# First attention: low and high halves of the values in one tile, two matmul passes, output products of a batch in one turn

## The reference, cut to what matters

```python
q = (x @ Wq.T).reshape(B, T, 16, 32).transpose(0, 2, 1, 3)      # k and v likewise; x is the layernorm of the input
att = einsum('bhtd,bhsd->bhts', q, k) / sqrt(32) + causal_mask
w = softmax(att, axis=-1)
z = einsum('bhts,bhsd->bhtd', w, v).transpose(0, 2, 1, 3).reshape(B, T, D)
x = x + z @ Wo.T
```

## Time and profile before

| | |
|---|---|
| median of 3 runs | 1908.64 us (1906.13 to 1909.9) |
| profiled execution, its own time | 1907.17 us |
| its span | 1905.7 us |
| TensorE busy in it | 1805.5 us (95%) |
| VectorE / ScalarE / GpSimd busy | 1113.3 / 807.4 / 1010.0 us |
| mean granted TensorE clock | 0.986 |
| first attention | from 0 to 250.7 us of the span; its loop from 34.2 us on |

### The profile page before, as it was taken

The page is one execution under the profiler, slowest core; times in us unless marked ns, Lnnn a source line. Parts: engine busy times, 40 slices in busy tenths (PEclk is TensorE's granted clock), DMA queues, the critical chain, the costliest instruction groups (busy, mean ns, idle before and its releaser), DMA issues. The chain is left out here.

```text
span 1905.7 us, 30804 instructions
## 1 busy us (share of the span) xinstructions
PE 1805.5 (95%) x10161; PEld 1565.8 (82%) x10167; DVE 1113.3 (58%) x2769; ACT 807.4 (42%) x2063; POOL 1010.0 (53%) x965
## 2 busy tenths in 40 slices
PE   7999989999999999999888999999999999999996
PEld 5888858788999999899667888888888888867795
DVE  6676785763333333335766666666666757566345
ACT  3767633222222222221256566666665433543231
POOL 3444341397883957895457456456453203116783
PEclk9999999999999999999999999999999999999998
DMA  3556430236653645554343234233331210012666
GB/s 116 173 155 205 144 138 0 78 145 226 231 199 126 214 144 180 191 153 127 90 112 95 68 92 117 57 89 93 84 78 56 74 50 1 24 50 84 213 214 195
DMA packets 104551, 232.54 MB, mean 122 GB/s; under 512 B 20672, under 2 KB 20928, under 8 KB 101328
## 3 DMA queue, kind: packets, MB, share of 16 engines
q1 hardware_dynamic: 84080, 144.31, 25.0%
q0 software_dynamic: 19744, 85.47, 13.6%
q10 hardware_dynamic: 576, 0.79, 0.2%
HBM read 126.23 MB, written 57.93 MB: 97 GB/s over the span
## 5 line engine op out<-in xcount | busy, mean ns | idle before, releaser
L712 POOL TENSOR_SCALAR a_E<-a_E,a_inv 128x128 f32<-128x128 f32 (+3 forms) x384 | 213.9, 575 | 237.7 <-DVE a_inv L848 237.7
L745 ACT ACTIVATE a_E<-a_E,a_top 128x512 f32<-128x512 f32 (+3 forms) x384 | 211.1, 565 | 6.0 <-DVE a_top L842 5.9
L153 PE MATMUL bank<-f_UH,f_XH 128*128 x596 | 200.5, 336 | 8.4 <-POOL f_UL L165 3.4
L153 PE MATMUL bank<-f_UL,f_XH 128*128 x596 | 193.2, 324 | 0.0
L153 PE MATMUL bank<-f_UH,f_XL 128*128 x596 | 193.2, 324 | 0.0
L842 DVE CUSTOM_DVE_ANT_0 a_E<-a_causal,bank 128x512 f32<-128x512 bf16 (+3 forms) x384 | 163.6, 480 | 43.0 <-PE bank L1023 31.5
L153 PE MATMUL bank<-a_PHL,a_VH 128*128 128x512 f32 (+3 forms) x768 | 181.1, 325 | 0.9 <-issue 0.6
L737 ACT ACTIVATE a_PHL<-bank 128x512 fp32r<-128x512 f32 (+1 forms) x288 | 131.0, 528 | 112.6 <-PE bank L1039 112.5
L1821 ACT ACTIVATE f_HH<-bank 128x256 fp32r<-128x256 f32 x220 | 59.8, 323 | 232.2 <-PE bank L2218 232.1
L165 DVE TENSOR_TENSOR a_PHL<-bank,a_PHL 128x512 fp32r<-128x512 f32 (+1 forms) x288 | 153.2, 585 | 5.1 <-ACT a_PHL L737 4.8
L1876 DVE TENSOR_TENSOR f_gate<-bank,f_gate 128x352 f32<-128x352 f32 x79 | 41.3, 522 | 192.1 <-PE bank L153 192.0
(11 more groups left out here) (407 smaller groups left out, 4864.8 us busy)
## 6 DMA issues: line engine op xcount, KB each, us to landing
f_uraw<-f_up POOLq DMA_DIRECT2D x18, 1408.0 KB, 6.7
f_xb<-table SPq DMA_DIRECT2D x86, 256.0 KB, 3.2
table<-f_ob SPq DMA_DIRECT2D x86, 256.0 KB, 2.7
table<-a_zeros SPq DMA_DIRECT2D x31, 512.0 KB, 4.3
f_draw<-f_down POOLq DMA_DIRECT2D x27, 512.0 KB, 4.5
a_g<-a_f SPq DMA_DIRECT2D x160, 64.0 KB, 2.0
a_raw<-a_qkv SPq DMA_DIRECT2D x36, 256.0 KB
f_uraw<-f_up POOLq DMA_DIRECT2D x9, 704.0 KB, 4.4
```

Of the source, the lines that this page charges most:

```text
L153: m = pe.matmul(out, a, b, start=first and i == 0 and j == 0, stop=last and i == n - 1 and j == 2, skip_group_check=not check)
L712: e.tensor_scalar(self.E[sl][:, a], self.E[sl][:, a], self.inv[:, sl, i:i + 1], 0.0, ALU.mult, ALU.add).then_inc(*self.s_nrm.up(N, m - 1, i))
L745: x = e.activation(E, E, ACT.Exp, scale=-1.0, bias=self.top[:, sl, i:i + 1], accum_out=self.total[:, sl, i:i + 1])
```

## The change

- The low part of a head's values no longer has a tile of its own: it goes into the same tile `VH`, 64 columns away from the high part. One matmul with this tile gives both the high values' and the low values' product, in different rows of the bank. So the values take two passes (`PH`, `PL`) in place of three. (The product low x low comes with it.)
- Heads 0 and 1 have rows 0 to 63, heads 2 and 3 rows 64 to 127; the other half of the bank holds their low products. So the bank is emptied after every second head, by ScalarE with two copies of 64 rows (`QH`, and `S` from the other half), a turn later by VectorE with a low part into `R`, and after the fourth head GpSimd adds `R + S` into `QL`.
- VectorE's low part moves from the end of turn m (job m-3) to turn m (job m-4), behind the reciprocal and ahead of `PL`. GpSimd's addition stands ahead of its normalizing instructions.
- The projected values are staged in a tile of their own (`W`).
- `FILL`: all four output products of a batch go into the turn of "T"; before, they stood in pairs in the two turns behind it. Output weights are split in turn 0 of the next step, not in turn 6; the queries' weights are loaded 2 turns ahead, not 4.
- The memset of `VL` goes for this attention. The second attention (heads 64 wide) keeps the old form.

```diff
+        self.beside = 4 * hd <= P
+        self.VH = sb("VH", [heads, NT, P], F32R)
+        if self.beside:
+            self.VL, self.HALF = self.VH, P // 2
+            self.S, self.R, self.W = sb("S", [T]), sb("R", [T]), sb("W", [T])
...
-            self.FILL = [[("P", K, 1), ("O", 0, -1), ("O", 1, -1)], [("P", 0, 1), ("O", 2, -1), ("O", 3, -1)],
-                         [("P", V, 1)], [("T", 1)], [("P", K, 0, 1), ("O", 4, -1), ("O", 5, -1)],
-                         [("P", 0, 0, 1), ("O", 6, -1), ("O", 7, -1)], [("P", V, 0, 1)], [("T", 0, 1)]]
-            self.SPLIT = {2: (K, 1), 3: (0, 1), 5: (V, 1), 6: (self.wt, 0)}
-            self.LEAD = {K: 3, 0: 4, V: 2, self.wt: 2}
+            self.FILL = [[("P", K, 1)], [("P", 0, 1)], [("P", V, 1)],
+                         [("T", 1)] + [("O", g, -1) for g in range(TT)],
+                         [("P", K, 0, 1)], [("P", 0, 0, 1)], [("P", V, 0, 1)],
+                         [("T", 0, 1)] + [("O", g, -1) for g in range(TT, NT)]]
+            self.SPLIT = {0: (self.wt, -1), 2: (K, 1), 3: (0, 1), 5: (V, 1)}
+            self.LEAD = {K: 3, 0: 2, V: 2, self.wt: 2}
...
-        for z in (self.VH, self.VL):
+        for z in (self.VH,) if self.beside else (self.VH, self.VL):
             e.memset(z[:, :, :, :].bitcast(F32), 0.0)
...
+            if self.beside and 4 <= m < self.M + 4 and self.jobs[m - 4][3] == self.heads - 1:
+                j, b, r, h = self.jobs[m - 4]
+                e.wait_ge(*self.s_olo.after(N, j, r, b, self.half(h)))
+                e.tensor_tensor(self.QL[:, r, b * T:b * T + T], self.R[:, :], self.S[:, :], ALU.add).then_inc(
+                    *self.s_rest.up(N, j, r, b))
...
-            if 3 <= m < self.M + 3 and self.jobs[m - 3][3] == self.heads - 1:
+            if 3 <= m < self.M + 3 and self.closes(self.jobs[m - 3][3]):
                 j, b, r, h = self.jobs[m - 3]
+                own, bank = self.rows(h), self.k.bank[self.OB]
                 e.wait_ge(*self.s_av.after(N, m - 3))
-                e.activation(self.QH[:, r, b * T:b * T + T], self.k.bank[self.OB][:, :], ACT.Copy).then_inc(
-                    *self.s_ohi.up(N, j, r, b))
+                x = e.activation(self.QH[own, r, b * T:b * T + T], bank[own, :], ACT.Copy)
+                if self.beside:
+                    if m - 3 >= self.heads:
+                        e.wait_ge(*self.s_rest.after(N, *self.outputs_before(m - 3)))
+                    x = e.activation(self.S[own, :], bank[self.other_rows(h), :], ACT.Copy)
+                x.then_inc(*self.s_ohi.up(N, j, r, b, self.half(h)))
...
+            if self.beside and 4 <= m < self.M + 4 and self.closes(self.jobs[m - 4][3]):
+                self._dve_low_values(m - 4)
...
-                t = product(e, self.k.bank[self.OB][:, sblk * P:T],
-                            [(self.VH[:, h, b * TT + sblk, :], self.VL[:, h, b * TT + sblk, :])],
-                            [(self.PH[m % 2][:, a], self.PL[m % 2][:, a])],
-                            first=h == 0 and sblk == 0, last=h == self.heads - 1 and ci == 2)
+                V, p = (b * TT + sblk), m % 2
+                passes = [(self.VH[:, h, V, :], self.PH[p][:, a]), (self.VH[:, h, V, :], self.PL[p][:, a])]
+                if not self.beside:
+                    passes.append((self.VL[:, h, V, :], self.PH[p][:, a]))
...
-        if h == self.heads - 1:
-            emptied[self.OB] = self.s_olo.after(N, j, r, b)
+        if self.closes(h):
+            emptied[self.OB] = self.s_olo.after(N, j, r, b, self.half(h))
```

More of the change, by code:

```diff
@@ L507, in split @@
             c, ahead = self.SPLIT[n]
-            if j + ahead < self.STEPS:
+            if 0 <= j + ahead < self.STEPS:
                 of.append((j + ahead, c))
@@ L544, in plan @@
         self.slot, self.free, self.fill_bank, self.score_bank = {}, {}, {}, {}
-        freed, ring, self.staged = [[], []], 0, {}
+        freed, turned, ring, self.staged = [[], []], [], 0, {}
         for m in self.loops:
@@ L563, in plan @@
                             continue
+                    if c == self.vt and self.beside:
+                        self.staged[j, b], self.free[x[1:]] = self.W[:, :], turned
+                        turned = [self.s_vt.after(N, j, b)]
+                        continue
                     s = self.slot[x[1:]] = len(self.slot) % 2
@@ L595, in plan @@
                 self.s_av.plan((N, m))
-                if h == self.heads - 1:
-                    self.s_ohi.plan((N, j, r, b))
-                    self.s_olo.plan((N, j, r, b))
+                if self.closes(h):
+                    self.s_ohi.plan((N, j, r, b, self.half(h)))
+                    self.s_olo.plan((N, j, r, b, self.half(h)))
+                if self.beside and h == self.heads - 1:
+                    self.s_rest.plan((N, j, r, b))
     def moves(self, j, c, b):
@@ L614, in moves, with half, opens, closes @@
                 [(self.KH[up, 1, a], g[dn, :]), (self.KH[dn, 1, a], g[dn, :]), (self.KL[dn, 1, a], f[dn, :])]]
+    def half(self, h):
+        return h * self.hd // self.HALF
+    def opens(self, h):
+        return h * self.hd % self.HALF == 0
+    def closes(self, h):
+        return (h + 1) * self.hd % self.HALF == 0
+    def rows(self, h):
+        return slice(self.half(h) * self.HALF, (self.half(h) + 1) * self.HALF)
+    def other_rows(self, h):
+        return slice((1 - self.half(h)) * self.HALF, (2 - self.half(h)) * self.HALF)
+    def low_columns(self, cs):
+        if not self.beside:
+            return cs
+        at = (cs.start + self.HALF) % P
+        return slice(at, at + self.hd)
+    def outputs_before(self, m):
+        j, b, r, h = self.jobs[m - self.heads]
+        return j, r, b
+    def outputs_low(self, j, b):
+        if self.beside:
+            return self.s_rest.after(self.name, j, self.queries[-1], b)
+        return self.s_olo.after(self.name, j, self.queries[-1], b, self.half(self.heads - 1))
     def out_weights(self, x, r):
@@ L866, in dve, with _dve_low_values @@
                 self._dve_low_rotated(m - 1)
[L867 to L872, removed]
+            if not self.beside and 3 <= m < self.M + 3 and self.closes(self.jobs[m - 3][3]):
+                self._dve_low_values(m - 3)
+    def _dve_low_values(self, m):
+        e, N, (j, b, r, h) = self.k.dve, self.name, self.jobs[m]
+        own, a, key = self.rows(h), slice(b * T, b * T + T), (N, j, r, b, self.half(h))
+        e.wait_ge(*self.s_ohi.after(*key))
+        if self.beside and m >= self.heads:
+            e.wait_ge(*self.s_rest.after(N, *self.outputs_before(m)))
+        to = self.R[own, :] if self.beside else self.QL[own, r, a]
+        low_part(e, to, self.k.bank[self.OB][own, :], self.QH[own, r, a]).then_inc(*self.s_olo.up(*key))
     def _stats(self, loaded, tiles):
@@ L995, in _pe_fill @@
                 if g % TT == 0:
-                    e.wait_ge(*self.s_olo.after(N, j, self.queries[-1], g // TT))
+                    e.wait_ge(*self.outputs_low(j, g // TT))
                 a = slice(g * P, g * P + P)
@@ L1049, in _pe_values @@
             e.wait_ge(*self.s_vlo.after(N, j, b))
-        if h == 0 and self.OB in emptied:
+        if self.opens(h) and self.OB in emptied:
             e.wait_ge(*emptied[self.OB])
@@ L1055, in _pe_values @@
                 a = slice(self.P_AT[sblk], self.P_AT[sblk] + T - sblk * P)
-                t = product(e, self.k.bank[self.OB][:, sblk * P:T],
-                            [(self.VH[:, h, b * TT + sblk, :], self.VL[:, h, b * TT + sblk, :])],
-                            [(self.PH[m % 2][:, a], self.PL[m % 2][:, a])],
-                            first=h == 0 and sblk == 0, last=h == self.heads - 1 and ci == 2)
+                V, p = (b * TT + sblk), m % 2
+                passes = [(self.VH[:, h, V, :], self.PH[p][:, a]), (self.VH[:, h, V, :], self.PL[p][:, a])]
+                if not self.beside:
+                    passes.append((self.VL[:, h, V, :], self.PH[p][:, a]))
+                for x, (values, weights) in enumerate(passes):
+                    t = e.matmul(self.k.bank[self.OB][:, sblk * P:T], values, weights,
+                                 start=self.opens(h) and sblk == 0 and x == 0,
+                                 stop=self.closes(h) and ci == 2 and x == len(passes) - 1)
         t.then_inc(*self.s_av.up(N, m))
-        if h == self.heads - 1:
-            emptied[self.OB] = self.s_olo.after(N, j, r, b)
+        if self.closes(h):
+            emptied[self.OB] = self.s_olo.after(N, j, r, b, self.half(h))
     def projections_done(self):
```

7 lines of the change are left out of this document (5 added, 2 removed).

## The result

The changed kernel takes 1915.34 us in the median (13 runs, 1907.89 to 1917.29), the kernel before beside it 1908.5 us (13 runs). The ratio is 1.0036, with a 95% interval of 1.0024 to 1.0047: slower by 6.8 us. The profiled execution took 1916.62 us around a span of 1915.4.

A forecast was written before the change was run, and what follows sets the result against it. TensorE was taken to bound the first attention's loop. Gains of 2.7 (four full groups), 1.2 (up to 105 us), 1.0 (end) and 0.1 (start) sum to 5.0 us, giving 1903.6 us; range 1895 to 1912.

The forecast's parts named there:

- The bound: First attention's loop: TensorE sets the pace, busy 26.7 of 27 us at full clock; removed matmuls gain until the next engine limits.
- the third pass: Values' product in each turn: the four VL matmuls go, 0.63 us each, 20.3 us of TensorE's issue over 32 turns.
- The short turn: Turn that turns the values: the fourth product waits for their bank, freed by VL; turn 8.45 or 9.04 us, some 2.6 waiting.
- the first kind: First short turn of a step, keeping the queries' weight copy (0.59): fourth product starts at +7.1 us, turn 9.04.
- the S copy: Second ScalarE copy of 64 partitions in the outputs' evacuation: taken as 0.49 us, with 0 and 1.0 as ends.
- The clock: Short turn's new wait of 2.3 to 2.9 us: forecast A had the clock hold, 1903.6 us, chance 0.45.
- right at the first kind: New wait of 2.3 to 2.9 us likened to idle times of 2.65 and 2.70 us, after which the clock was not full.
- rival C: Clock falls at all five short-turn waits and stays low through the next projection, 2.3 us each; 1915 us, chance 0.14.
- the query weights' load: Sync queue in the first step: this load now stands ahead of the query moves, costing 0.5 us.
- The first step: Turns from 54.33 to 78.44, without products: 0.63 us less each, counted as 2.7 us gained up to 78.44.
- The tail: From turn 28 to the stage's end: 37.4 us against 38.4, gain 1.0, possibly a loss of 3.
- The start: Removed memset of VL: TensorE's first projection waits for YL on VectorE, not GpSimd; gain 0 to 0.2 us, taken as 0.1.

The follow-up runs named there:

- after with two memsets: Changed kernel with two memsets of a spare tile on GpSimd at the start, where the memset of VL stood; ratio 1.0028.
- the kernel of 1895.67: Changed kernel with products ahead of turned values, weights loaded earlier and the next stage's fetch in turn 27 instead of 20; 1895.67 us, ratio 0.9935.
- both repairs of the loop: Changed kernel with eight constant matmuls ahead of each short turn's fourth product and earlier weight loads; 1907.85 us, ratio 1.0003.
- two memsets in the best kernel: The kernel of 1895.67 with two memsets of a spare tile on GpSimd at the start; ratio 0.9939.
- with the two repairs: Both repairs of the loop, here with two memsets of a spare tile on GpSimd at the start as well; ratio 1.0004.

## Why the prediction was wrong, step by step

**The bound.** Right: TensorE sets the pace in the loop. A turn with one projection takes 5.75 to 5.77 us, forecast 5.78; the third pass is worth its 0.63 a turn wherever nothing else is late.

**The short turn, without the clock.** Right, closely. The wait for the bank of the turned values is in all five short turns, put down to VL on VectorE. The fourth product starts 6.58 us after the turn's start at 128.75 (forecast 6.5), and in the first kind 7.70 us after 100.13 (forecast 7.1; 0.6 more, as the output weights come late). With the clock held and the loads early the turns are 8.66 and 9.17 (forecast 8.45 and 9.04), and four groups take the 104.3 us forecast. Against it, the S copy takes its full place (0.60 between QH and S, 0.62 to PH) rather than 0.49, some 0.2 us on that chain.

**The clock: the step that failed.** The text had both rows for it, waits of 2.65 and 2.70 with a fall and one of 1.50 without, put the new wait at 2.3 to 2.9 us "right at the first kind", and still gave the fall at all five 0.14, because TensorE is busy on both sides of the wait. Being busy around it did not help: the clock fell at each of the five, down to waits of 2.16 us, and again at each of the five in the profile of after with two memsets. Its price was less than rival C's 2.3 us each: with the loads early the five short turns take 10.51, 10.13, 10.54, 9.46 and 10.21 us, and with the waits filled as well 9.18, 8.66, 9.16, 8.67 and 8.67. That is 1.3 to 1.5 for each of the four with a fall; the one of 9.46 had none, and most of its 0.8 is the wait for moved queries. Where the low clock reaches the next turn, up to 0.65 more (turns of 6.40 and 6.27 instead of 5.75). From turn 8 to 28 filling the waits brought 7.4 us in after and 6.8 with the loads early. C's 2.3 us came from the matmuls at 36.51, taken as the first fall lasting on. Three stretches of before (columns of the earlier trace rows) show two falls, with the full clock between them:

```profile
28.40:31.70 3.30, 2.82 (x12) 2.42 (x12) 0.62 (x2) 0.80 (x2) 0.00 (x0) 0.50 0.81 199
31.80:35.10 3.30, 1.78 (x11) 1.30 (x11) 3.30 (x9) 2.06 (x7) 0.00 (x0) 1.00 0.42 150
35.20:38.50 3.30, 3.11 (x7) 2.38 (x8) 2.22 (x9) 2.07 (x7) 0.00 (x0) 0.50 0.02 5
```

The rule in the Trainium skill, "TensorE: Matmul & The Clock Gate", section "HAM oscillation — how this bites in real kernels", that a loop can pay a fall in each iteration, is what the trace shows here. The page's example waits some 3 to 5 us each time; here waits of 2.16 us had a fall too.

**What was not looked at: the loads behind the query moves.** The forecast costed the query weights' load ahead of the moves, 0.5 us, and this was right: turn 1 to turn 4 takes 14.88 us instead of 14.32. It did not ask what stands behind the moves. The output weights, now split in turn 0 of the next step, are loaded behind 12 moves of some 0.6 us each, and ScalarE waits 13.8 us for them in three places, 3.9 us for other weights in three more. What it adds: a fourth product that waits 3.27 and 3.55 us instead of 2.68, a turn 9 of 7.15 instead of 5.75, and most of what the first step lost (next point). Alone its repair brought 1.0036 - 1.0015 = 0.2%, some 4 us, with intervals that overlap; together with the clock 0.33%, some 6.3, and there the intervals lie apart.

**The first step.** Forecast: 2.7 us gained by turn 8, measured 0.4 (38.4 to 38.0). Turn 4 takes 7.22, as before, although the pass that went is worth 0.63. Its clock is full (1.00 from 52 to 70 us). Behind its wait for the moves, which grew from 0.44 to 2.20, stands a second one of 1.10 (0.52 in before) for the bank of the turned values, and ahead of both ScalarE had waited for the queries' weights:

```profile
54.59 0.63 ACT L844 ACTIVATE a_WH<-a_raw 128x512 fp32r<-128x512 f32 x1 [2.35 <-DMA a_raw<-a_qkv]
60.36 0.47 PE L153 MATMUL bank<-YH,a_WH 128*128 128x512 f32 x1 [1.10 <-DVE a_VH L164]
```

With the loads ahead both ScalarE's wait and the second wait are gone, turn 4 takes 5.87, and turn 1 to turn 8 takes 36.2, 1.9 of the 2.3 us that were missing. The short turn without products takes 4.42 instead of 3.47: its values start at 79.04 behind 0.73 us of idle time, 0.10 after the low part `R` has left the outputs' bank (the trace names no releaser). That low part was moved a turn later, and the prediction booked only what that relieves.

**The tail.** Forecast 37.4, measured 37.7, with VectorE's additions 1.32 us apart (the six gaps from 252.24 to 260.15) as it said. The gain of 0.8 is there.

**The start.** That TensorE's first projection waits for YL and not for GpSimd is true, but looked one step too late: the chain to YL begins with a centring on VectorE which GpSimd, free of its memset, now holds up. Forecast 0.1 gained, measured 2.4 us lost at turn 1: 1.2 at the first scores, of which the late transposes are 0.24 and the rest goes with a longer idle time and the low clock behind it, and 1.2 in turn 0, which stays open. On the SBUF side the Trainium skill, "SBUF — State Buffer", section "🔬 SBUF: two separate sides", says that VectorE and GpSimd share one pair of ports as an exclusive lock, held for a whole instruction by whoever starts first, where VectorE runs in a mode that uses both ports or, against a GpSimd instruction that reads SBUF, takes two inputs from SBUF. In which mode the centring runs no row tells. The rows of the kernel of 1895.67 agree: the centring that starts 0.27 us after GpSimd lasts 1.28 us and ends at 12.24, behind GpSimd's instruction that began at 10.69.

**The sum.** The stage's forecast end was 245.7, the measured 260.88. The 15.2 us lie in: start 2.4, first step 2.3, turns 8 to 12 2.8, turns 12 to 28 7.4, tail 0.3. Falls of the clock and late loads share the loop's part of it. With both repairs of the loop the time from turn 1 to the end is 206.4 us, against 210.7 in before and 205.7 forecast, and the eight matmuls too many in turn 31 are in it. Of the rivals, C gave the mechanism and the sign. That its 1915 is the time measured is partly chance: its price for a fall was too high, and the late loads and the start, which no rival had, made up for it. The range of 1895 to 1912 missed the time because it held C only by half and the loads not at all.

## What to carry to other kernels

Before work is gathered into one turn, list the banks it takes in order and ask who frees each: where the last entry of a turn needs the bank that the first one took, swapping the entries can repair it, worth 0.55% here. Cost a new idle stretch of TensorE by the nearest rows of waits and the clock behind them, and if the wait is as long as one that ends in a low clock, count that as the likely case. When a load's issue turn changes, read the queue for what now stands ahead of it and for what is removed in front of other engines, even where an engine's end is far from any bound.

## What the runs showed of the hardware

- In the loop, TensorE's waits for the turned values' bank had half the clock in or behind them in 6 of 6 cases at 2.68 to 3.62 us, in 8 of 10 at 2.16 to 2.19, and in 2 of 4 at 1.90 to 1.93. Waits for moved queries had it before turn 24 at 2.03 and 2.28, and at turn 4 in none of four at 2.19 to 2.22 and in one of seven at 1.65 to 1.67. Waits of up to 1.43 for a bank in the short turns, with and without constant matmuls ahead, had none. In between the same wait can go either way.
- At the start, idle times up to 1.94 us left the clock at 1.00 in seven profiles, those from 2.25 us on had 0.83 in seven. The wait of 2.65 us before the transposes at 28 to 30.5 us stands in all fourteen; in twelve half the clock came with it, in two (two memsets in the best kernel, and with the two repairs) it did not.
- Eight constant matmuls (1.90 us) ahead of each of the five waits kept the clock at 1.00 and took 7.4 us off turns 8 to 28 in the profile; eight more in a turn without a wait cost some 0.7 to 1.1.
- A ScalarE copy of 64 rows into the other half's rows takes 0.59 us, as much as one on its own rows, and gives way to the next after 0.60 to 0.62; a copy of 128 rows takes 0.60. A low part of 64 rows and 512 columns on VectorE takes up to 0.69, one of 128 rows in before 0.69. Half the rows save next to nothing.
- A centring of 512 columns on VectorE takes 0.5 us alone and up to 1.49 us beside GpSimd's subtraction from tiles.
